# Three of eight experts' down products as three products of high and low parts

## The chip, the cores and the metric

The kernel runs on one core of a Trainium2 chip, as one launch. The time is the device time of that launch in microseconds (us). The core has five engines, each with a queue of its own that it works off in order: TensorE (PE in the profile, its weight loads PEld), VectorE (DVE), ScalarE (ACT), GpSimd (POOL) and SyncE (SP), which here issues DMA transfers. Engines wait for one another by semaphores.

## The reference

One transformer layer in float32: x has 8 sequences of 256 tokens of 128 features, 2048 tokens in all.

- Attention: 16 heads of 8 features, softmax over 256 keys, an output projection, added to x, layer norm: y.
- Feed-forward: a shared part, (silu(y sw1) * (y sw3)) sw2 with 256 hidden features, and a routed part. The router scores 8 experts by sigmoid(y router_w), takes the two best of each token and makes their scores sum to 1 (`comb`, zero for the other six). Each expert e is gelu(y ew1[e]) ew2[e], 128 by 128 and 128 by 128; the routed part is the sum over experts of comb[e] times that.
- y plus both parts, layer norm: the output.

Every expert is computed for every token; the gate `comb` is multiplied onto the hidden features before the second ("down") matrix.

## The kernel before, in words

**A written order.** `lay_out_slots` (L81) writes a list of slots, each with a list of jobs; every engine's program walks the same list and emits its own instructions for each job, so the list is the order in each engine's queue. The attention takes 64 slots with scores. What follows is the drain, which starts at about 135 us in the trace; "slot k" below is slot k of the drain (`NHALF + k` in the code), and "9 slots ahead of the drain" is `NHALF - 9`.

**Units.** The feed-forward works on groups of 512 tokens, g0 to g3, with features on the partitions. A unit is one group with one expert (g1E2: group 1, expert 2) or with one half of the shared hidden features. Slots 0 to 7 have two units each: g0E0 to g0E7, whose up products were made ahead of the drain, and, in this order, the shared halves of g0, g1 and g2, then g1E0 and g1E1. Slots 8 to 13 have g1E2 to g1E7, 14 and 15 the shared halves of g3, 16 to 23 g2E0 to g2E7, 24 to 29 g3E0 to g3E5, and 30 to 33 g3E6 and g3E7 by halves of 256 tokens.

**One expert unit.** TensorE makes the up product in a PSUM bank (`ring`, two in turn): three float32r products by `three` (L843), low weights with high activations, high with low, high with high. ScalarE takes gelu of it (L719), VectorE multiplies by the gates (L815) into one of four buffers `hid`, TensorE multiplies that by the down weights `wf` in float32 (L1050) and adds it to the group's accumulator in PSUM. For groups 0 to 2 this is one product of 512 columns; group 3's accumulator lies in two banks, so it is two of 256. The trace shows a float32 product as two instructions. The up product has to wait until gelu has read the unit that had its bank before, and `hid` until the down product of four units earlier is done.

**Where the down product stands.** For units of slots 0 to 7 in the next slot, after its up products; for the others two slots on, before that slot's up product.

**Jobs around it that the prediction names.**

- accT f, finT f, rstd2 f, norm2 f: group f is finished. ScalarE copies the accumulator (L726), TensorE transposes it (L1057) after that copy, VectorE adds y and makes the statistics (L822 to L829), GpSimd the reciprocal root (L574, L575), VectorE the normed output (L835), SP stores it. accT stands in slots 10, 16, 26, finT in 11, 17, 27, norm2 in 15, 21, 31 for f = 0, 1, 2; group 3 has two halves, f = 3 and 4, at the end. The statistics stand after the unit of their slot on VectorE.
- route, combT n, load gates n: group n's gates. GpSimd and VectorE make `comb`, TensorE transposes it (L1005), ScalarE copies it out of PSUM (L707), SP stores it to DRAM (L483) and loads it back, spread over all partitions, 2 MB (L478). combT stands in slots 7 and 18 and load gates in 8 and 19 for n = 2 and 3.
- ScalarE's exp (router, L701) needs another table than gelu and tanh: there are table loads before and after it, in slots 4 and 7.

`qstack` and `kstack` are the attention's operands and are not used in the drain.

Of the kernel before, what the change touches and what calls it, by code (L numbers as in the profile page):

```python
# [15 lines left out]
F32 = mybir.dt.float32  # L16
# [5 lines left out]
P = 128  # L22
# [39 lines left out]
WARM = 10  # L62

# [17 lines left out]
def lay_out_slots():  # L81
# [57 lines left out]
    for u, n in zip(EARLY, (53, 54, 55, 56, 58, 59, 61, 62)):  # L139
        put(n, ("up", u))  # L140

    for u in range(NUNITS):
        if UNIT_SLOT[u] >= NE:
            put(NHALF + UNIT_SLOT[u] + 2, ("down", u))
        put(NHALF + UNIT_SLOT[u], ("unit", u))
    for u in range(NUNITS):
        if UNIT_SLOT[u] < NE:
            put(NHALF + UNIT_SLOT[u] + 1, ("down", u))
# [49 lines left out]
def build_layer(nc, x, x_t, w_attn, w_first, b_first, b_rows, w_ffn, out):  # L198
    ctx = ExitStack()
    with ctx:  # L200
# [115 lines left out]
        up_copied = sem("up_copied")  # L316
        acc_taken, fin_stats, fin_rstd, fin_out = sem("acc_taken"), sem("fin_stats"), sem("fin_rstd"), sem("fin_out")
# [54 lines left out]
        def misc_of(u):  # L372
            return bank_of[u]

# [117 lines left out]
        def _(pool):  # L492
# [19 lines left out]
            for slot in slots:  # L512
                for kind, n in slot.jobs:
# [38 lines left out]
                    if kind == "add bo":  # L552
                        if n == 0:
                            wait_taken(pool, ("bo", 0))
                            pool.wait_ge(x_loaded, 16 * NG)
                        pool.tensor_tensor(xs[:, tiles(n), :], xs[:, tiles(n), :],
                                           bo_all[:, None, :].to_broadcast([P, TPG, P]), ALU.add).then_inc(xb_made, 1)
                    if kind == "y":
# [59 lines left out]
        def _(act):  # L618
# [10 lines left out]
            for slot in slots:  # L629
# [18 lines left out]
                for kind, b in slot.jobs:  # L648
# [59 lines left out]
                    if kind == "unit":  # L708
# [7 lines left out]
                        if b in SHARED:  # L716
                            nc.scalar.activation(act_out[:, b % 2, :], up[:, :], ACT.Tanh, scale=0.5).then_inc(act_made, 1)
                        else:
                            nc.scalar.activation(act_out[:, b % 2, c], up[:, c], ACT.Gelu).then_inc(act_made, 1)  # L719
                    if kind == "accT":  # L720
# [8 lines left out]
        def _(dve):  # L729
# [7 lines left out]
            for slot in slots:  # L737
# [10 lines left out]
                for kind, b in slot.jobs:  # L748
# [49 lines left out]
                    if kind == "unit":  # L798
# [13 lines left out]
                        else:  # L812
# [3 lines left out]
                                              gates_mem[:, g % 2, e * GT + c.start:e * GT + c.stop], ALU.mult).then_inc(hid_dve, 1)  # L816
                    if kind == "finT":
# [22 lines left out]
        def _(pe):  # L840
# [61 lines left out]
            for slot in slots:  # L902
# [25 lines left out]
                for kind, b in slot.jobs:  # L928
# [107 lines left out]
                    if kind == "down":  # L1036
# [10 lines left out]
                        if g == NG - 1 and b == first_of(g):  # L1047
                            pe.wait_ge(acc_taken, 1)
                        for bank, cols in acc_parts(g, cols_of(b)):
                            ins = mm(bank[:, cols], wf[:, c:c + P], hid[:, b % NHB, cols], start=b == first_of(g),  # L1050
# [52 lines left out]
```

## Time and profile before

| what | value |
|---|---|
| runs shown | 218.22, 219.63, 970.13 us; median 219.63 |
| profiled execution, its own time | 217.16 us |
| its span, first to last instruction | 215.3 us |
| mean granted clock of TensorE | 0.995 |
| busy: TensorE, VectorE, ScalarE, GpSimd | 93%, 72%, 64%, 60% of the span |
| chain that ended last, by engine | PE 66%, DVE 14%, POOL 6%, issue 5%, ACT 4% |

The profile is of one execution. Its own time is 1.9 us more than its span, which is what lies before the first and after the last instruction that is shown. One of the three runs took 970 us; the other two agree within 0.7%.

### The profile page before, as it was taken

The numbers are of one execution on the slowest core, as the hardware profiler recorded it, in microseconds if no ns is written. First come the engines' busy times: TensorE is split into PE (matmuls) and PEld (weight loads), VectorE is DVE, ScalarE is ACT, GpSimd is POOL, SyncE is SP. The second block draws the span as 40 slices with busy tenths as digits, with TensorE's granted clock in tenths as the row PEclk, the third lists the DMA queues.
The fourth block names the chain that finished last, engine by engine and source line by source line (L and its number), as shares of the span: only waits on it lengthen the run. The fifth ranks groups of instructions, "written<-read, shape, count | busy, mean of one in ns | idle before, by whom it ended". The sixth has DMA issues, their size and how long they took to land.

```text
span 215.3 us, 4566 instructions
## 1 busy us (share of the span) xinstructions
PE 201.1 (93%) x1564; PEld 118.5 (55%) x1564; DVE 155.1 (72%) x319; ACT 138.1 (64%) x280; POOL 128.8 (60%) x248
## 2 busy tenths in 40 slices
PE   7999999999999999999999999899999999999980
PEld 7765564444555555555555455556655656557750
DVE  6788888779898989999874343577582657663774
ACT  2799786887769778787886657734776424434330
POOL 8888999348679985975379344192570864300203
PEclk9999999999999999999999999999999999999998
DMA  4490474367420000000063002700003701290011
GB/s 139 129 270 24 109 228 114 87 198 257 110 68 9 0 9 2 9 0 3 6 243 161 3 0 84 313 0 0 0 0 88 307 0 36 65 386 6 0 52 49
DMA packets 10358, 19.19 MB, mean 89 GB/s; under 512 B 1920, under 2 KB 6912, under 8 KB 9696
## 3 DMA queue, kind: packets, MB, share of 16 engines
q1 hardware_dynamic: 8912, 17.06, 24.5%
q10 hardware_dynamic: 1040, 1.05, 1.5%
q0 software_dynamic: 384, 0.79, 1.4%
q8 instruction: 13, 0.21, 0.4%
q14 instruction: 9, 0.07, 0.1%
HBM read 12.80 MB, written 1.11 MB: 65 GB/s over the span
## 4 chain that ended last, share of the span: by engine, by line
PE 66%; DVE 14%; POOL 6%; issue 5%; ACT 4%; DMA 2%; POOLq 0%; DVEq 0%
PE pv_bank L893 11%; PE max_bank L1050 8%; PE ring L867 8%; DVE top L745 5%; PE sum_bank L1050 4%; PE sum_bank L867 3%; POOL qstack L428 3%; PE ring L845 2%; PE max_bank L876 2%; PE ring L847 2%; PE ring L846 2%; PE misc_bank L983 2%; PE pv_bank L901 2%; PE misc_bank L972 2%; PE misc_bank L845 2%
## 5 line engine op out<-in xcount | busy, mean ns | idle before, releaser
L745 DVE TENSOR_REDUCE top<-max_bank 128x2 f32<-128x512 f32 x128 | 80.6, 683 | 10.8 <-PE max_bank L876 10.8
L639 ACT ACTIVATE probs_mem<-ring 128x512 f32<-128x512 f32 x86 | 49.0, 599 | 15.7 <-PE ring L867 7.4
L876 PE MATMUL max_bank<-kstack,qstack 32*128 32x256 f32 x256 | 41.0, 328 | 0.3 <-DVE kstack L754 0.3
L893 PE MATMUL pv_bank<-probs_mem,v 128*18 128x256 f32 x512 | 40.1, 385 | 0.5 <-ACT probs_mem L639 0.2
L815 DVE TENSOR_TENSOR probs_mem<-xt,gates_mem 128x512 f32<-128x512 f32 (+1 forms) x34 | 22.7, 673 | 23.2 <-ACT xt L719 22.2
L867 PE MATMUL ring<-qstack,kstack 32*128 32x256 f32 x172 | 35.1, 326 | 1.7 <-DVE top L745 1.7
L639 ACT ACTIVATE probs_mem<-sum_bank 128x512 f32<-128x512 f32 x42 | 25.1, 598 | 7.5 <-PE ring L867 7.2
L719 ACT ACTIVATE xt<-ring 128x512 f32<-128x512 f32 (+1 forms) x26 | 14.7, 564 | 23.5 <-PE ring L847 23.5
L1050 PE MATMUL max_bank<-probs_mem,wf 128*128 128x512 f32 (+1 forms) x60 | 27.5, 541 | 1.3 <-DVE probs_mem L815 0.9
L876 PEld LDWEIGHTS max_bank<-kstack,qstack 32*128 32x128 f32 x256 | 25.4, 183 | 5.6 <-issue 2.5
L867 PEld LDWEIGHTS ring<-qstack,kstack 32*128 32x128 f32 x172 | 21.2, 183 | 13.3 <-issue 5.6
L845 PE MATMUL ring<-yt_hi,wf_lo 128*128 128x512 f32 (+1 forms) x34 | 22.0, 648 | 0.0
L867 PE MATMUL sum_bank<-qstack,kstack 32*128 32x256 f32 x84 | 20.7, 325 | 0.8 <-DVE top L745 0.4
L1050 PE MATMUL sum_bank<-probs_mem,wf 128*128 128x512 f32 (+1 forms) x40 | 15.9, 488 | 0.3 <-DVE probs_mem L815 0.3
L574 POOL TENSOR_SCALAR rstd<-mv 128x4 f32<-128x4 f32 (+1 forms) x5 | 1.9, 370 | 23.9 <-DVE mv L829 23.8
L867 PEld LDWEIGHTS sum_bank<-qstack,kstack 32*128 32x128 f32 x84 | 12.3, 183 | 6.1 <-ACT probs_mem L639 2.8
L569 POOL TENSOR_SCALAR yt_hi<-yt_raw 128x256 fp32r<-128x256 f32 x8 | 6.8, 852 | 13.1 <-ACT yt_raw L697 13.0
L1050 PEld LDWEIGHTS max_bank<-probs_mem,wf 128*128 128x128 f32 x60 | 9.7, 188 | 8.9 <-DVE probs_mem L815 4.4
L893 PEld LDWEIGHTS pv_bank<-probs_mem,v 128*18 128x18 f32 x512 | 8.6, 96 | 9.4 <-issue 0.7
L563 POOL TENSOR_SCALAR xs<-res,mv,rstd 128x128 f32<-128x128 f32 x16 | 12.7, 797 | 0.9
L847 PE MATMUL ring<-yt_hi,wf_hi 128*128 128x512 f32 (+1 forms) x34 | 13.0, 382 | 0.0
L846 PE MATMUL ring<-yt_lo,wf_hi 128*128 128x512 f32 (+1 forms) x34 | 13.0, 381 | 0.0
(183 smaller groups left out, 389.9 us busy)
## 6 DMA issues: line engine op xcount, KB each, us to landing
gates_mem<-gate_scratch SPq DMA_DIRECT2D x4, 2048.0 KB, 7.8
kstack<-gates_mem SPq DMA_DIRECT2D x36, 64.0 KB, 2.7
qstack<-gates_mem SPq DMA_DIRECT2D x24, 64.0 KB, 2.1
wf<-w_ffn_dram SPq DMA_DIRECT2D x1, 1408.0 KB, 7.3
xs<-x_dram SPq DMA_DIRECT2D x4, 256.0 KB, 5.6
xt<-x_t_dram SPq DMA_DIRECT2D x3, 256.0 KB, 4.4
qstack<-gates_mem POOLq DMA_DIRECT2D x12, 64.0 KB, 2.5
out_dram<-xs SPq DMA_DIRECT2D x3, 256.0 KB, 2.3
```

The lines of the kernel that those rows point to most:

```text
L563: ins = pool.tensor_scalar(xs[:, QT * n + t, :], res1[:, t, :], mv1[:, t, 0:1], rstd1[:, t:t + 1], ALU.subtract, ALU.mult)
L639: nc.scalar.activation(probs[:, i % 2, s_heads(s)[r], :], ring_of["scores", 2 * s + r][:, :], ACT.Exp, scale=SCALE).then_inc(probs_made, 1)
L719: nc.scalar.activation(act_out[:, b % 2, c], up[:, c], ACT.Gelu).then_inc(act_made, 1)
L745: dve.tensor_reduce(top[:, b % 2, m_heads(m)[r], t, :], max_bank[(2 * m + r) % NMAX][:, :].rearrange("p (h k) -> p h k", h=2), AX.X, ALU.m ...
L815: dve.tensor_tensor(hid[:, b % NHB, c], act_out[:, b % 2, c], gates_mem[:, g % 2, e * GT + c.start:e * GT + c.stop], ALU.mult).then_inc(hi ...
L845: mm(out_ap, w_lo, m_hi, start=first, stop=False)
L846: mm(out_ap, w_hi, m_lo, start=False, stop=False)
L847: return mm(out_ap, w_hi, m_hi, start=False, stop=last)
L867: ins = mm(ring_of["scores", 2 * s + r][:, kt * S:(kt + 1) * S], kstack[rows, t, k:k + P], qstack[rows, t, b * S:(b + 1) * S], start=True, ...
L876: ins = mm(max_bank[(2 * m + r) % NMAX][:, qt * S:(qt + 1) * S], qstack[rows, t, q:q + P], kstack[rows, t, b * S:(b + 1) * S], start=True, ...
L893: ins = mm(pv_bank[32 * j:32 * j + 2 * VW, 0:S], v[:, (QT * b + kt) * H // 2 + HPS * n + j, k * VW:(k + 2) * VW], probs[:, p // 2 % 2, j, ...
L1050: ins = mm(bank[:, cols], wf[:, c:c + P], hid[:, b % NHB, cols], start=b == first_of(g), stop=b in [fin_last(f) for f in range(len(FIN))])
```

## The change

Experts 0, 2 and 4 (`IN_PARTS`) are treated otherwise in all four groups, which makes twelve units (`PARTED`): slots 0, 2, 4 of g0; 6, 8, 10 of g1; 16, 18, 20 of g2; 24, 26, 28 of g3.

- Their down weights are split by GpSimd into a float32r high part and the rest, 128 columns for each expert, in three jobs ("split w2") 9, 7 and 5 slots ahead of the drain; the parts lie in `qstack`.
- Their hidden features are split too ("parts", after the last unit of the same slot): ScalarE waits for the gate product and copies it as float32r, VectorE waits for that copy and subtracts it from the product. The parts lie in `kstack`, two buffers in turn.
- Their down product is `three`: three float32r products in place of one in float32, per bank. TensorE waits for the subtraction before it.
- Their down product stands three slots on instead of two where it stood two on; in slots 1 to 7 it stands where it did.

```diff
@@ -60,6 +60,9 @@
 COPIES = ((1, 0, 0), (0, 0, 1))
 NC = 4
 WARM = 10
+
+IN_PARTS = (0, 2, 4)
+PARTED = tuple(u for u in range(NWHOLE) if UNITS[u][1] - NSH in IN_PARTS)
 
 SHIFT_D = (0, 4)
 NDIRECT = 2 * NT
@@ -138,11 +141,17 @@
                 put(first + 34 - 3 * (b // 2), ("load gates", b // 2))
     for u, n in zip(EARLY, (53, 54, 55, 56, 58, 59, 61, 62)):
         put(n, ("up", u))
+    for n in range(len(IN_PARTS)):
+        put(55 + 2 * n, ("split w2", n))
 
     for u in range(NUNITS):
         if UNIT_SLOT[u] >= NE:
-            put(NHALF + UNIT_SLOT[u] + 2, ("down", u))
+            put(NHALF + UNIT_SLOT[u] + (3 if u in PARTED else 2), ("down", u))
         put(NHALF + UNIT_SLOT[u], ("unit", u))
+        last = u if u + 1 == NUNITS or UNIT_SLOT[u + 1] > UNIT_SLOT[u] else None
+        for w in PARTED:
+            if last is not None and UNIT_SLOT[w] == UNIT_SLOT[last]:
+                put(NHALF + UNIT_SLOT[w], ("parts", w))
     for u in range(NUNITS):
         if UNIT_SLOT[u] < NE:
             put(NHALF + UNIT_SLOT[u] + 1, ("down", u))
@@ -314,6 +323,7 @@
         up_made, act_made, sh_read, hid_dve, down_made = (
             sem("up_made"), sem("act_made"), sem("sh_read"), sem("hid_dve"), sem("down_made"))
         up_copied = sem("up_copied")
+        w2_hi_made, w2_split, hid_hi_made, hid_lo_made = sem("w2_hi_made"), sem("w2_split"), sem("hid_hi_made"), sem("hid_lo_made")
         acc_taken, fin_stats, fin_rstd, fin_out = sem("acc_taken"), sem("fin_stats"), sem("fin_rstd"), sem("fin_out")
         out_stored = sem("out_stored")
 
@@ -371,6 +381,14 @@
 
         def misc_of(u):
             return bank_of[u]
+
+
+        def w2_part(e, i):
+            n = IN_PARTS.index(e)
+            return qstack[:, i, n * P:(n + 1) * P]
+
+        def hid_part(u, i):
+            return kstack[:, 2 * (PARTED.index(u) % 2) + i, 0:GT]
 
 
         def acc_parts(g, cols):
@@ -555,6 +573,14 @@
                             pool.wait_ge(x_loaded, 16 * NG)
                         pool.tensor_tensor(xs[:, tiles(n), :], xs[:, tiles(n), :],
                                            bo_all[:, None, :].to_broadcast([P, TPG, P]), ALU.add).then_inc(xb_made, 1)
+                    if kind == "split w2":
+                        if n == 0:
+                            pool.wait_ge(up_made, 1)
+                        e = IN_PARTS[n]
+                        c = slice(E2 + e * P, E2 + (e + 1) * P)
+                        pool.tensor_scalar(w2_part(e, 0), wf[:, c], 1.0, None, ALU.mult).then_inc(w2_hi_made, 1)
+                        pool.wait_ge(w2_hi_made, n + 1)
+                        pool.tensor_tensor(w2_part(e, 1), wf[:, c], w2_part(e, 0).bitcast(F32), ALU.subtract).then_inc(w2_split, 1)
                     if kind == "y":
                         pool.wait_ge(stats_made, n + 1)
                         chain(pool.tensor_scalar(rstd1[:, :], mv1[:, :, 1], EPS, None, ALU.add))
@@ -717,6 +743,12 @@
                             nc.scalar.activation(act_out[:, b % 2, :], up[:, :], ACT.Tanh, scale=0.5).then_inc(act_made, 1)
                         else:
                             nc.scalar.activation(act_out[:, b % 2, c], up[:, c], ACT.Gelu).then_inc(act_made, 1)
+                    if kind == "parts":
+                        n = PARTED.index(b)
+                        wait_hid(act, b)
+                        if n >= 2:
+                            act.wait_ge(down_made, PARTED[n - 2] + 1)
+                        nc.scalar.copy(hid_part(b, 0), hid[:, b % NHB, :]).then_inc(hid_hi_made, 1)
                     if kind == "accT":
                         g, t0, t1 = FIN[b]
                         act.wait_ge(down_made, fin_last(b) + 1)
@@ -814,6 +846,10 @@
                             e, c = n - NSH, cols_of(b)
                             dve.tensor_tensor(hid[:, b % NHB, c], act_out[:, b % 2, c],
                                               gates_mem[:, g % 2, e * GT + c.start:e * GT + c.stop], ALU.mult).then_inc(hid_dve, 1)
+                    if kind == "parts":
+                        dve.wait_ge(hid_hi_made, PARTED.index(b) + 1)
+                        dve.tensor_tensor(hid_part(b, 1), hid[:, b % NHB, :], hid_part(b, 0).bitcast(F32),
+                                          ALU.subtract).then_inc(hid_lo_made, 1)
                     if kind == "finT":
                         g, t0, t1 = FIN[b]
                         dve.wait_ge(misc_made, made[kind, b])
@@ -1046,7 +1082,15 @@
                         c = W2 + n * P
                         if g == NG - 1 and b == first_of(g):
                             pe.wait_ge(acc_taken, 1)
+                        if b in PARTED:
+                            e = n - NSH
+                            pe.wait_ge(w2_split, len(IN_PARTS))
+                            pe.wait_ge(hid_lo_made, PARTED.index(b) + 1)
                         for bank, cols in acc_parts(g, cols_of(b)):
+                            if b in PARTED:
+                                ins = three(bank[:, cols], w2_part(e, 0), w2_part(e, 1), hid_part(b, 0)[:, cols],
+                                            hid_part(b, 1)[:, cols], b == first_of(g), False)
+                                continue
                             ins = mm(bank[:, cols], wf[:, c:c + P], hid[:, b % NHB, cols], start=b == first_of(g),
                                      stop=b in [fin_last(f) for f in range(len(FIN))])
                         ins.then_inc(down_made, 1)
```

## Rows read from the trace of the kernel before

**Rows 1.** the page's busy time, share of the span and instructions.
```profile
PE 201.1 (93%) x1564; PEld 118.5 (55%) x1564; DVE 155.1 (72%) x319; ACT 138.1 (64%) x280; POOL 128.8 (60%) x248
```

**Rows 2.** stages: PE, PEld, DVE, ACT, POOL busy, then clock, DMA, GB/s.
```profile
190.00:200.00 10.00, 10.00 (x42) 6.72 (x41) 5.38 (x11) 4.06 (x7) 0.00 (x0) 1.00 0.35 134
...
210.00:215.30 5.30, 0.07 (x1) 0.00 (x0) 2.25 (x9) 0.00 (x0) 1.89 (x4) 0.82 0.17 49
```

**Rows 3.** chain of waits in the drain: start us, us, what.
```profile
149.34 0.23 PE ring L846
...
150.50 0.86 PE sum_bank L1050 x2
...
181.77 0.44 PE pv_bank L1057 x4
...
195.60 0.51 PE max_bank L1050 x2
...
196.11 0.43 PE sum_bank L1050 x2
...
204.00 0.12 PE ring L846
```

**Rows 4.** groups by line and shape, 135 to 208: busy us, mean ns.
```profile
L719 ACT ACTIVATE xt<-ring 128x512 f32<-128x512 f32 x22 | 13.1, 597 | 20.3 <-PE ring L847 20.2
...
L719 ACT ACTIVATE xt<-v 128x512 f32<-128x512 f32 x5 | 3.2, 630 | 0.6 <-DVE probs_mem L815 0.5
...
L726 ACT COPY xt<-max_bank 128x512 f32<-128x512 f32 x2 | 1.2, 580 | 0.0
```

**Rows 5.** gate product, by its line: duration ns min/median/max.
```profile
L815 DVE TENSOR_TENSOR probs_mem<-xt,gates_mem x34: 421/691/1222, 136.7 to 207.9; 128x512 f32<-128x512 f32 x30, 128x256 f32<-128x256 f32 x4
```

**Rows 6.** weight split's first instruction, by its line.
```profile
L532 POOL TENSOR_SCALAR wf_hi<-wf x16: 441/449/461, 53.3 to 79.8; 128x96 fp32r<-128x96 f32 x16
```

**Rows 7.** timeline of POOL ahead of the drain: start, us, idle before.
```profile
129.98 0.22 POOL L560 TENSOR_SCALAR rstd<-mv 128x2 f32<-128x2 f32 x1 [3.13 <-DVE mv L782]
```

**Rows 8.** timeline of ACT, slots 7 and 8: start, us.
```profile
158.21 0.63 ACT L719 ACTIVATE xt<-v 128x512 f32<-128x512 f32 x1 [0.54 <-DVE probs_mem L815]
...
159.98 1.28 ACT L701 ACT_TABLE_LOAD   x1
...
164.37 0.60 ACT L719 ACTIVATE xt<-ring 128x512 f32<-128x512 f32 x1
```

**Rows 9.** waits in the drain: us in total, times, longest.
```profile
PE max_bank L1050 <- DVE probs_mem L815: 0.9, 3, 0.4
```

**Rows 10.** timeline of ACT and DVE, slots 15 and 16.
```profile
180.23 0.58 ACT L726 COPY xt<-max_bank 128x512 f32<-128x512 f32 x1
...
180.31 1.09 DVE L835 TENSOR_SCALAR xs<-xt,mv,rstd 128x128 f32<-128x128 f32 x4
...
181.31 0.69 DVE L815 TENSOR_TENSOR probs_mem<-xt,gates_mem 128x512 f32<-128x512 f32 x1
```

**Rows 11.** timeline of DVE, ACT and SP, slots 17 to 24.
```profile
183.04 0.69 DVE L822 TENSOR_TENSOR xt<-pv_bank,xs 128x512 f32<-128x512 f32 x1
...
184.40 0.56 ACT L707 COPY comb_t<-misc_bank 8x512 f32<-8x512 f32 x1
...
184.97 0.66 DVE L815 TENSOR_TENSOR probs_mem<-xt,gates_mem 128x512 f32<-128x512 f32 x1
...
186.50 0.33 SPq L478 DMA_DIRECT2D gates_mem<-gate_scratch  x1
...
194.67 0.69 DVE L815 TENSOR_TENSOR probs_mem<-xt,gates_mem 128x512 f32<-128x512 f32 x1 [0.95 <-ACT xt L719]
```

**Rows 12.** stages: the slice in which the last gate load's traffic ends.
```profile
194.00:194.50 0.50, 0.50 (x3) 0.26 (x2) 0.00 (x0) 0.47 (x1) 0.00 (x0) 1.00 0.08 25
```

**Rows 13.** timeline of POOL and DVE, slot 6.
```profile
157.66 1.05 POOL L570 TENSOR_TENSOR yt_lo<-yt_raw,yt_hi 128x256 fp32r<-128x256 f32 x1
...
158.03 1.22 DVE L815 TENSOR_TENSOR probs_mem<-xt,gates_mem 128x512 f32<-128x512 f32 x1
```

## The prediction

> **What bounds the kernel now.** I read the page's busy time first [rows 1]: TensorE 93% of the span, no other engine above 72%. The table by stage [rows 2] shows where that holds in the stretch the change touches, the drain (135 us to the end): in 190 to 200 TensorE has no idle time, ScalarE works 4.1 us, VectorE 5.4, GpSimd nothing. The chain of waits [rows 3] then gives the size of a step, because it counts a pipelined product once: a float32 down product of 512 columns is 0.86 us, in group 3 (two halves) 0.51 + 0.43 = 0.94; a float32r product is 0.23 for 512 columns and 0.12 for 256. So TensorE's queue is what ends last, but with thin cover: a slot of the drain is one up product (0.70) and one down product (0.86), about 1.6 us, and in that time the unit's chain has to run gelu (0.60) and gate product (0.69) [rows 4, 5]: 1.3 us. Whatever is put between those two engines is put near the path.
>
> **The change, part by part.**
>
> *Removed from TensorE.* Twelve down products become three float32r products each. Nine (groups 0 to 2) go from 0.86 to 3 x 0.233 = 0.70: 9 x 0.16 = 1.4 us. Three (group 3) go from 0.94 to 6 x 0.117 = 0.70: 0.7 us. If TensorE never waited for it, 2.2 us. [rows 3]
>
> *Added.* ScalarE: 12 copies, SBUF to SBUF, 512 columns. The trace has a copy from PSUM at 0.58 and an activation from SBUF at 0.63 [rows 4]; I take 0.60, and 0.58 to 0.63 moves nothing. VectorE: 12 subtractions of two SBUF operands, as the gate product has them, whose median is 0.69 and whose longest is 1.22 [rows 5]; I take the median and keep the longest as the upper end. GpSimd: three weight splits of two instructions; a 96-column one takes 0.45 [rows 6], so 2 x 0.45 x 128/96 = 1.2 us a split. They stand 9, 7 and 5 slots ahead of the drain, before the last batch's normalisation, where GpSimd waits 3.13 us [rows 7]; TensorE asks for them only in the drain. I cost them at nothing; if all three fell into that one gap they would overrun it by 0.5 us, which is the upper end. No DMA is added.
>
> *Moved.* From slot 8 on the parted unit's down product stands in slot +3, so even slots have one up product and no down product, odd slots two. The hidden buffer is reused four units later, after that slot: no wait. The new wait on TensorE is for the subtraction. The wait that matters is the other one: **ScalarE waits for the gate product before its copy, in the middle of its queue**, and behind the copy stand the next gelu, and in slots 10, 16 and 26 the copy of a finished accumulator (accT), in slot 18 the copy of the last group's gates (combT 3). TensorE's transposes (finT) wait for the first, the gate load for the second.
>
> I carried the four queues forward slot by slot, with 0.60 for ScalarE, 0.69 for VectorE, 0.03 to 0.05 for a hand-over and 0.5 or 0.6 for two independent instructions back to back. Where it stands against before:
>
> a) Slots 0 to 7. Both up products of a slot (1.4 us) precede the downs, so copy and subtraction are hidden; three parted units give 0.45 us. In slot 6 half goes back: g1E0's copy can start only after its gate product (about 159.1), ending at 159.7; then gelu g0E7 (158.21 before), gelu g1E1 (two at 0.5 pitch), a table load of 1.28, exp (0.2), the gate copy (0.6) and a second load of 1.28 follow on ScalarE, with hand-overs 4.4 us, and gelu g1E2 comes at 164.1 against 164.37 [rows 8]. Standing: -0.2 us.
>
> b) Slots 8 to 14. g1E2: gelu to 164.7, gate product 165.5, copy 166.1, subtraction 166.8; TensorE is there at 166.0 and idles 0.8. accT 0 behind g1E4's copy costs 0.3. Against that 0.3 of saved products and two of the three old waits of 0.9 together [rows 9]. Standing: +0.1.
>
> c) Slot 17. VectorE norms group 0 at 180.31 for 1.09 us, so g2E0's gate product comes at 181.31 already today, and ends at 182.0 [rows 10]. accT 1, today at 180.23, must now follow the copy behind that: 181.4 + 0.69, copy to 182.7, accT to 183.2. finT 1 was issued at 181.77 [rows 3]; TensorE arrives at 181.85 and waits until 183.27. This is the clearest single cost: 1.4 us. Standing: +1.5.
>
> d) Slots 18 to 24. finT 1's residual and statistics take VectorE from 183.04 to 184.97 [rows 11] and stand before g2E2's gate product; its copy and subtraction end 1.4 us after that. TensorE waits about 0.5 and 0.35, and regains 0.5 by three cheaper products and 0.2 in bubbles. Standing: +1.6.
>
> e) The last gates. combT 3's copy stands behind g2E2's copy, which waits for (d): 187.5 instead of 184.40, 3.1 us later. Store and load follow: the load goes out at 186.50 and its traffic ends in the slice 194.0 to 194.5 [rows 11, 12]; the first product that reads it starts at 194.67, 0.4 us of slack. The load moves 3.1, the stream only 1.6: 3.1 - 1.6 - 0.4 = 1.1 us. Standing: +2.7.
>
> f) Slots 24 to the end. accT 2's wait stays hidden behind the late gates. finT 2's 1.93 us on VectorE stand before g3E4's gate product, copy and subtraction: TensorE idles 1.35 in slot 31, 0.3 elsewhere, and saves 0.7. Standing at the end: **+3.6 us**.
>
> The profiled execution took 217.16 us, so it would take 220.8. The median of the runs shown, 219.63, lies 2.5 above the profiled run and the lowest 1.1 above; with the middle, 1.8, I forecast 222.5.
>
> **A rule against the trace.** The longest gate product, 1.22 us, began at 158.03, inside a GpSimd subtraction that ran from 157.66 for 1.05 [rows 13]; the median met no such thing, so in the sum each subtraction is 0.69. The Trainium skill (SBUF — State Buffer, section Who interferes with whom) says that a VectorE instruction with two SBUF inputs and a GpSimd instruction that reads SBUF shut each other out: the second to issue waits for the first. By that rule, which these two rows agree with, the subtractions of slots 6 to 20 are all exposed; with 0.5 us more for each of the three of slots 16 to 20 alone the sum would be an estimated +5.1 in place of +3.6.
>
> **Rivals.**
>
> *The ScalarE-VectorE loop becomes the bound (ends slower).* For a pair of slots the loop is gate product, copy, subtraction, gate product: 3 x 0.69 + 0.60 and hand-overs, 2.8 us; TensorE's pair is 0.70 + 0.86 + 2 x 0.70 = 2.96. It decides when one step costs 0.2 us more than I took. A subtraction blocked as in [rows 13] costs 0.5 more; over six pairs of groups 2 and 3, with 0.3 us lost in each, 2 us: +5.6, or 224.6. For it: the margin is 5%. Against it: GpSimd does nothing in 190 to 200 [rows 2], so only slots 16 to 21 are exposed. Chance 0.20.
>
> *All savings are collected.* 217.16 - 2.2 = 215.0, as a median 216.8. For it: TensorE is the bound by every view, and slots 0 to 5 hide the additions. Against it: (c) needs no assumption on prices, only the order on ScalarE. Chance 0.10.
>
> *Only the waits of (b) and (c) stay.* If combT 3's copy slips by less than 2 us the gates arrive in time, and the finer waits vanish in the slots without a down product: about +1.5, 220.5. Chance 0.20.
>
> *TensorE's clock.* The granted clock is 1.00 in the drain and 0.82 only in the last slice, where TensorE hardly works [rows 2]; new idle stretches are at most 1.4 us. If it fell there, 3 us of products at half speed would cost 3 more: 225.5. Chance 0.05.
>
> **How the numbers follow.** Forecast 0.45, its own range +1.5 to +5.5 us, 219.7 to 225.1 with the two offsets. The range down to the third rival and most of the second, up to the first and the clock: 218.2 to 226.3. What this kernel's measurement can tell from no change is about 2%, 4.4 us. Faster by more than that is out of reach of 2.2 us of savings: 0.02. Slower: the first rival and the clock, and a quarter of the forecast's own chance: 0.33. Within: 0.65.
>
> **What would show it.** In the profile after: parted downs as three L845 to L847-like products of 0.23 (else the saving is wrong); ScalarE's copies beginning just after a gate product, and accT 1 after one; idle time of TensorE before finT 1 of a microsecond or more, named for ScalarE (if under 0.3, (c) is wrong); the last gate load issued near 189.6 and a gate product waiting for it (if issued before 188, (e) is wrong); TensorE's idle time before the parted downs of g1E2 and g3E4 named for VectorE. A shorter span than 215 us would refute the whole reading.

## The result, and the profile after

The changed kernel took 223.14 us (median of six runs) where the kernel before took 218.17 on the same chip: ratio 1.0204, 95% interval 1.0158 to 1.0251, so 3.4 to 5.5 us slower. The ratio leaves out the executions at a lower granted clock (two of the six, 225.70 and 227.65 us), so it is not the quotient of the two medians. The forecast was 222.5, of which the last step, from the profiled execution to a median, was 0.8 too large: before's median lay 1.0 above its profiled run here, not 1.8. The work itself was forecast at +3.6. The interval of the runs contains that; the two profiled executions, compared below, show more.

The spans differ by 5.9 us, but not all of that is the change's. ScalarE's first tanh of the drain starts at 136.99 us before and at 137.78 after. That start varied from 136.72 to 139.11 over the kernels below, and did not follow the edits: e5 and e10 run the same code up to there and start at 139.11 and 136.72. From there to the end of the span it is 78.3 us before and 83.4 after: **the drain is 5.1 us longer**. All lengths of the drain below are counted this way.

The page's busy time, and two stages of the table by stage (columns as in [rows 2]), of the changed kernel:

```profile
PE 201.2 (91%) x1579; PEld 120.5 (54%) x1579; DVE 163.2 (74%) x331; ACT 144.2 (65%) x292; POOL 132.9 (60%) x254
...
190.00:200.00 10.00, 9.71 (x32) 5.63 (x32) 5.82 (x12) 4.06 (x8) 0.00 (x0) 1.00 0.65 238
210.00:221.20 11.20, 4.95 (x27) 3.53 (x25) 5.62 (x21) 1.79 (x5) 1.89 (x4) 0.90 0.16 47
```

Against [rows 1, 2]: the granted clock is 1.00 in every stage from 140 to 210, as it was before, so the clock is not it. TensorE's busy time did not fall, although its products got shorter: a float32r product of 512 columns counts about 0.39 in busy time and 0.23 in the chain. The chain of waits of the changed kernel, from g2E0's gate product to g3E0's down product, the first in three products in group 3 (start us, us, what):

```profile
183.28 0.61 DVE probs_mem L847
183.92 0.02 ACT kstack L751
184.44 0.58 ACT xt L758
185.02 0.51 ACT xt L745
...
186.16 0.70 DVE xt L858
...
189.31 0.57 ACT comb_t L733
...
191.41 7.54 DMA gates_mem<-gate_scratch
199.07 0.70 DVE probs_mem L847
...
201.64 0.12 PE max_bank L882
```

Where TensorE carried this stretch of the chain before [rows 3], VectorE, ScalarE and the gate load carry it now. L751 is ScalarE's copy of the high part, L758 accT, L745 gelu, L733 the copy of combT, L847 the gate product, L851 the subtraction, L858 finT's addition of y. The timeline of ScalarE for units g2E0 and g2E1 (slots 16 and 17), with the idle time before an instruction and its releaser in brackets:

```profile
181.62 0.60 ACT L745 ACTIVATE xt<-ring 128x512 f32<-128x512 f32 x1 [1.29 <-PE ring L883]
183.92 0.62 ACT L751 CAST kstack<-probs_mem 128x512 fp32r<-128x512 f32 x1 [1.70 <-DVE probs_mem L847]
184.44 0.58 ACT L758 COPY xt<-max_bank 128x512 f32<-128x512 f32 x1
184.92 0.60 ACT L745 ACTIVATE xt<-ring 128x512 f32<-128x512 f32 x1
```

The copy stands idle 1.70 us in the middle of ScalarE's queue for a gate product that is itself behind VectorE's norm of group 0; accT 1 and the next gelu stand behind it. The second gelu waits for no one: its up product had ended 1.3 us before, at 183.65. Before, gelu g2E1 started at 181.81 and had waited for TensorE. The waits of the drain, us in total, times, longest, first of the changed kernel, then two of the kernel before:

```profile
ACT xt L745 <- PE ring L883: 12.8, 12, 2.3
ACT kstack L751 <- DVE probs_mem L847: 12.4, 10, 2.1
DVE kstack L851 <- ACT kstack L751: 6.2, 9, 0.7
PE max_bank L881 <- DVE kstack L851: 5.0, 5, 1.6
PE pv_bank L1101 <- ACT xt L758: 2.1, 2, 1.5
DVE probs_mem L847 <- DMA gates_mem<-gate_scratch: 1.5, 1, 1.5
```
```profile
ACT xt L719 <- PE ring L847: 23.5, 24, 1.5
PEld max_bank L1050 <- DVE probs_mem L815: 4.4, 12, 0.8
```

A gelu that waits for its up product is in time: 24 were before, 12 are now. The last row, of the kernel before, is one that the prediction missed: before the change TensorE's weight loads for the down products already waited 12 times, 4.4 us, for the gate product. [rows 9] shows only the part of it that is booked on the products themselves, 0.9.

### The profile page after: what moved, and what is told of

Same layout as the page of the kernel before. It is cut to its first block, busy times and chain, and to the rows that moved or that the text cites. A ratio compares the mean times of both kernels' runs of the same rounds, so it can differ in the third digit from the quotient of the medians.

```text
span 221.2 us, 4648 instructions
## 1 busy us (share of the span) xinstructions
PE 201.2 (91%) x1579; PEld 120.5 (54%) x1579; DVE 163.2 (74%) x331; ACT 144.2 (65%) x292; POOL 132.9 (60%) x254
## 3 DMA queue, kind: packets, MB, share of 16 engines
q10 hardware_dynamic: 1040, 1.05, 1.4%
## 4 chain that ended last, share of the span: by engine, by line
PE 59%; DVE 20%; ACT 9%; issue 6%; DMA 3%; ACTq 1%; POOLq 0%; POOL 0%; DVEq 0%
PE pv_bank L929 12%; PE ring L903 8%; DVE top L777 5%; DMA gates_mem<-gate_scratch 3%; DVE probs_mem L847 3%; PE sum_bank L903 3%; PE max_bank L912 3%; PE pv_bank L937 2%; PE sum_bank L1094 2%; PE misc_bank L1019 2%; PE max_bank L1094 2%; PE max_bank L881 2%; ACT xt L745 2%; PE ring L980 2%; PE misc_bank L1008 2%
## 5 line engine op out<-in xcount | busy, mean ns | idle before, releaser
L847 DVE TENSOR_TENSOR probs_mem<-xt,gates_mem 128x512 f32<-128x512 f32 (+1 forms) x34 | 22.5, 675 | 15.4 <-ACT xt L745 13.9
L745 ACT ACTIVATE xt<-ring 128x512 f32<-128x512 f32 (+1 forms) x26 | 14.2, 561 | 13.5 <-PE ring L883 12.8
L1094 PE MATMUL max_bank<-probs_mem,wf 128*128 128x512 f32 (+1 forms) x42 | 19.3, 540 | 0.9 <-DVE probs_mem L847 0.6
L881 PE MATMUL ring<-yt_hi,wf_lo 128*128 128x512 f32 (+1 forms) x34 | 19.7, 579 | 0.0
L751 ACT CAST kstack<-probs_mem 128x512 fp32r<-128x512 f32 x12 | 7.4, 618 | 12.4 <-DVE probs_mem L847 12.4
L851 DVE TENSOR_TENSOR kstack<-probs_mem,kstack 128x512 fp32r<-128x512 f32 x12 | 8.4, 702 | 6.2 <-ACT kstack L751 6.2
```

The costliest lines, as they stand in the source:

```text
L847: dve.tensor_tensor(hid[:, b % NHB, c], act_out[:, b % 2, c], gates_mem[:, g % 2, e * GT + c.start:e * GT + c.stop], ALU.mult).then_inc(hi ...
L881: mm(out_ap, w_lo, m_hi, start=first, stop=False)
```

## The experiments

One table for all. "At" is the start of a unit's gelu or tanh in ScalarE's timeline, minus its start before, both counted from the first tanh of the drain; "end" is the same for the end of the span. So a column shows how late the stream runs there, and the step between two columns is what that stretch cost.

| kernel | ratio to before (95%) | at g1E0 | g1E2 | g3, 1st shared | g2E3 | g3E0 | g3E4 | end |
|---|---|---|---|---|---|---|---|---|
| changed | 1.0204 (1.0158 to 1.0251) | 0.08 | 0.37 | 1.09 | 3.09 | 3.05 | 3.32 | 5.1 |
| e1 parts last | 1.021 (1.0173 to 1.0247) | 0.85 | 1.08 | 1.82 | 2.98 | 3.19 | 2.86 | 4.7 |
| e2 products only | 0.9938 (0.9899 to 0.9976) | -0.32 | -0.73 | -0.89 | -1.05 | -1.08 | -1.20 | -1.15 |
| e3 no last gates | 1.0233 (1.0205 to 1.026) | 0.11 | 0.38 | 1.09 | 3.08 | 3.05 | 2.76 | 4.6 |
| e4 pairs later | 1.0075 (1.0041 to 1.0108) | 0.86 | 0.61 | 0.83 | 2.32 | 1.98 | 1.64 | 2.05 |
| e5 parts unused | 1.0228 (1.0166 to 1.0291) | 0.44 | 0.11 | 0.93 | 2.95 | 2.91 | 4.46 | 4.8 |
| e6 parts next | 1.0176 (1.0097 to 1.0255) | 0.85 | 0.80 | 2.74 | 1.57 | 4.22 | 4.09 | 4.0 |
| e7 copy on VectorE | 1.0125 (1.0073 to 1.0177) | 0.29 | 0.53 | 0.91 | 1.71 | 2.30 | 1.81 | 3.4 |
| e8 only g0 | 0.9964 (0.9927 to 1.0001) | 0.09 | -0.40 | -0.38 | -0.35 | -0.38 | -0.39 | -0.3 |
| e9 subtraction only | 1.002 (0.9978 to 1.0061) | 0.03 | 0.25 | 0.36 | 0.40 | 0.60 | 0.56 | 0.8 |
| e10 copy only | 1.0185 (1.0134 to 1.0236) | 0.44 | 0.11 | 0.93 | 2.95 | 2.91 | 4.53 | 4.8 |
| e11 pairs later, parts last from slot 8 | 1.0021 (0.999 to 1.0052) | 0.08 | -0.11 | 0.11 | 1.59 | 1.24 | 0.91 | 1.2 |
| e12 the same, copy on VectorE | 1.0005 (0.9968 to 1.0042) | 0.30 | 0.53 | 0.58 | -0.14 | 1.03 | 0.60 | 0.4 |

The last column comes from one profiled execution each, the ratio from several runs. Taken times 218 us, each ratio's excess lies within 0.9 us of the last column; differences of 0.5 us are read from the columns, not from the ratios.

**e1, the parts behind accT and combT.**

```diff
+    for slot in slots:
+        slot.jobs.sort(key=lambda job: job[0] == "parts")
```

> Edit: within a slot the two instructions that make the parts go to the end of the slot's list, behind accT 0 to 2 and the copy of combT 3; nothing else is changed. Theory (written order on ScalarE): the copy of the high part waits 1.6 us for a gate product, and accT 1, then finT 1, and the copy of combT 3 with the last gates' load stand behind it; freed of that, finT 1 waits nothing (1.5 less) and the last load is issued 2 to 3 us earlier, so the wait of 1.5 us on it goes: 2.0 to 2.5 us faster than the changed kernel, about 220.7 us where the kernel before takes 218.2 (ratio 1.01). Rival (the twelve subtractions' and copies' hand-over between ScalarE and VectorE costs by itself, whatever stands behind it): within 0.5 us of the changed kernel, ratio 1.018 to 1.022.

Measured: ratio 1.021, as slow as the changed kernel; drain 0.4 shorter. My first theory, 2.0 to 2.5 us, was far too large. Its waits:

```profile
PE max_bank L883 <- DVE kstack L853: 5.3, 5, 1.6
PE pv_bank L1103 <- ACT xt L760: 0.6, 1, 0.6
```

finT's wait for accT did go, 2.1 to 0.6 us, and with it the stretch from the g3 units to g2E3 costs 1.2 in place of 2.0. But in the slots 0 to 5 the parts now stand behind the attention's last jobs and come late there: +0.77 at g1E0. TensorE's waits for the subtraction stayed (5.3 against 5.0). The edit took one wait off the stream and put another on.

**e2, the products without the parts.**

```diff
-            put(NHALF + UNIT_SLOT[u] + (3 if u in PARTED else 2), ("down", u))
+            put(NHALF + UNIT_SLOT[u] + 2, ("down", u))
...
-                put(NHALF + UNIT_SLOT[w], ("parts", w))
...
-                            pe.wait_ge(hid_lo_made, PARTED.index(b) + 1)
```

> Leaves out the making of the parts in the drain (the products read what lies in the tiles, so the sums are not the reference's); the twelve down products are still three products each and stand two slots behind their unit, as the float32 ones did. It shows what TensorE alone gains. Theory: 2.2 us faster than the kernel before (9 times 0.16 and 3 times 0.24), as TensorE waits little there: about 216.0 us, ratio 0.990. Rival (the three products save nothing, since TensorE's busy time in the drain did not shrink in the changed kernel, 201.2 against 201.1 us): ratio 1.00, and then waits alone did not cause the loss.

Measured: ratio 0.9938, drain 1.15 shorter. The products are cheaper, but only half of 2.2 us is collected. It comes in g0 and g1 (-1.08 at g1E7); the six units of g2 and g3 bring 0.1 to 0.3. Starts of TensorE's second instruction of each up product in slots 20 to 23, of e2 and then of before:

```profile
186.87 0.40 PE L881 MATMUL ring<-yt_lo,wf_hi 128*128 128x512 f32 x1
188.48 0.40 PE L881 MATMUL ring<-yt_lo,wf_hi 128*128 128x512 f32 x1
189.94 0.40 PE L881 MATMUL ring<-yt_lo,wf_hi 128*128 128x512 f32 x1
191.72 0.40 PE L881 MATMUL ring<-yt_lo,wf_hi 128*128 128x512 f32 x1
```
```profile
186.88 0.40 PE L846 MATMUL ring<-yt_lo,wf_hi 128*128 128x512 f32 x1
188.48 0.40 PE L846 MATMUL ring<-yt_lo,wf_hi 128*128 128x512 f32 x1
190.12 0.40 PE L846 MATMUL ring<-yt_lo,wf_hi 128*128 128x512 f32 x1
191.72 0.40 PE L846 MATMUL ring<-yt_lo,wf_hi 128*128 128x512 f32 x1
```

The slot with the parted product is 1.46 us in place of 1.64, the next one 1.78 in place of 1.60: the 0.18 goes into waiting for the next gate product. So before the change two slots of g2, 3.2 us, were as long as TensorE's work in them and, within 0.2 us, as long as the round of up product, gelu, gate product and down product, which also takes two slots.

**e3, no load of the last gates.**

```diff
+                        if n == NG - 1:
+                            continue
...
-                            dve.wait_ge(gates_loaded[g % 2], 16 * (g // 2 + 1))
+                            dve.wait_ge(gates_loaded[g % 2], 16 * (min(g, 1) // 2 + 1) if g != 2 else 32)
```

> Leaves out the load of the last group's gates and the wait for it: the last group is weighted with the gates of group 1. Theory: VectorE's wait of 1.51 us for that load before g3E0's gate product is lost time, so 1.2 to 1.5 us less than the changed kernel: ratio to the kernel before 1.014. Rival (something else is as late there, the copy of g2E4's part or accT 1): the gate product waits for its gelu instead and the end moves by under 0.4 us: ratio 1.019 to 1.021.

Measured: ratio 1.0233, no gain; in the table the stream is 0.57 earlier from g3E1 on and 0.5 at the end. The load's wait of 1.51 is in the trace, but only 0.5 of it is on the path: without it g3E0's gate product waits for the copies and gelus that are late anyway. That is the rival, nearly to its number (under 0.4).

**e4, the downs of a pair one slot later.** As e1, and:

```diff
-            put(NHALF + UNIT_SLOT[u] + (3 if u in PARTED else 2), ("down", u))
+            put(NHALF + UNIT_SLOT[u] + (4 if u in PARTED else 3 if u - 1 in PARTED else 2), ("down", u))
...
-            put(NHALF + UNIT_SLOT[u] + 1, ("down", u))
+            put(NHALF + UNIT_SLOT[u] + (2 if u in PARTED and u not in EARLY else 1), ("down", u))
```

> Edit: the parts at the end of their slot as in the first kernel of this set, and the down products of a parted unit, and of the unit behind it, one slot later still (g1E0's too). Theory: TensorE then also stops waiting for VectorE's subtraction in the drain (five waits of 5.0 us together in the changed kernel), of which some 3 us are on the path: 3 us beyond the first kernel of this set, about 217 to 218 us, ratio 0.995 to 1.0. Rival (ScalarE and VectorE are the bound with the parts in, so waits only move to the gelus and the gate products): no better than the first kernel of this set by more than 0.5 us, ratio 1.008 or above.

Measured: ratio 1.0075, drain 2.65 shorter than e1's. That is nearly the 3 us of the theory, from a level that was 2 us higher than the theory's. TensorE's five waits for the subtraction (5.3) are gone, one of 0.4 is left, and a new one comes in:

```profile
ACT kstack L753 <- DVE probs_mem L849: 10.4, 9, 2.4
PE ring L883 <- ACT xt L747: 2.4, 4, 1.3
PE sum_bank L883 <- DVE kstack L853: 0.4, 1, 0.4
```

The up product now waits for a bank that a late gelu has not read yet. ScalarE's copy still waits 10.4 us for gate products.

**e5, the parts made and not used.** TensorE's code is that of before:

```diff
-            put(NHALF + UNIT_SLOT[u] + (3 if u in PARTED else 2), ("down", u))
+            put(NHALF + UNIT_SLOT[u] + 2, ("down", u))
...
-                        if b in PARTED:
+                        if False:
...
```

> The parts are made as in the changed kernel, in the same places of ScalarE's and VectorE's lists, but nobody reads them: the twelve down products are the float32 ones of before, two slots behind their unit, and wait for the gate product alone. Theory now (the two instructions per unit hold up the next gelu and the next gate product on their own engines, since ScalarE's copy waits for a gate product and VectorE's subtraction for that copy): most of the loss stays, ratio to the kernel before 1.012 to 1.020. Rival (the loss is TensorE's waiting for the subtraction, five waits of 5.0 us): with nobody waiting for it, 1.000 to 1.004.

Measured: ratio 1.0228, drain 4.8 longer. **Nearly the whole loss is there while nobody waits for a part.** So most of it needs no waiting of TensorE for the subtraction, though these five waits are TensorE's largest by name in the changed kernel. It comes from what stands in ScalarE's and VectorE's queues. That does not make the five waits free: e5 gives up the cheaper products too. The parts alone cost 4.8 and the products alone save 1.15 (e2), which makes +3.65; the changed kernel stands at +5.1. The 1.5 between belongs to neither alone. TensorE's waits for the parts, which only the changed kernel has, are its likely cause; that is not shown.

**e6, the parts one slot later.** As e4, and the jobs go behind the next unit:

```diff
-                put(NHALF + UNIT_SLOT[w], ("parts", w))
+                put(NHALF + UNIT_SLOT[w] + (w not in EARLY), ("parts", w))
```

> Edit: from slot 6 of the drain on, the copy and the subtraction of a unit stand one slot later, behind the gelu and the gate product of the next unit, and the downs as in the fourth kernel (both of a pair four slots behind the first). The work is the same. Theory (an engine that waits in order for the other is what costs): ScalarE's copy finds its gate product made and VectorE's subtraction does not hold up the next gate product; 1.5 to 2.5 us faster than the fourth kernel (1.0075), ratio 0.996 to 1.001. Rival (the added busy time, 7.4 us of ScalarE and 8.4 us of VectorE, is itself the cost): no better than the fourth kernel, 1.006 to 1.009.

Measured: ratio 1.0176, slower than e4 (1.0075). ScalarE's waits for a gate product ahead of its copies fell from 10.4 to 1.2 us, and it did not help: that theory, as I put it, fell. The table says where: 1.9 us of the difference to e4 are there by the g3 units. The chain of waits of e6:

```profile
163.26 0.02 ACT comb_t L735
...
163.75 0.62 ACT kstack L753
164.39 0.70 DVE kstack L853
...
165.23 0.47 PE max_bank L883
```

g1E0's copy, at the end of slot 7, now stands behind the copy of group 2's gates, which waits for GpSimd's routing. From there to the end e6 and e4 lose the same, 1.3 and 1.2. So up to the g3 units this run compares another place with another neighbour. Behind them ScalarE's copies wait 7.5 us in e4 and 0.9 in e6, for the same loss: with the downs where both kernels have them, these waits by themselves do not set the pace.

**e7, VectorE makes both parts.**

```diff
-                        nc.scalar.copy(hid_part(b, 0), hid[:, b % NHB, :]).then_inc(hid_hi_made, 1)
...
+                        dve.tensor_scalar(hid_part(b, 0), hid[:, b % NHB, :], 1.0, None, ALU.mult).then_inc(hid_hi_made, 1)
```

> Edit: VectorE makes the high part too (a copy with rounding ahead of its subtraction), ScalarE has no part in it; places in the lists and slots as in the changed kernel. Theory (the hand-over is the cost): VectorE's waits for ScalarE's copy (6.2 us in 9 waits) and ScalarE's waits for the gate product (12.4 us) go, the gelus stand as before, and VectorE has some 0.35 to 0.7 us more per unit: ratio 1.005 to 1.014. Rival (VectorE's own work ahead of the next gate product is the cost): it grows by 12 times 0.35 to 0.7 us, ratio 1.022 to 1.035.

Measured: ratio 1.0125, drain 1.7 shorter than the changed kernel's, with 5.2 us more work on VectorE (12 copies of 0.43). It is work for the busier engine, but ScalarE no longer waits in mid-queue for a gate product of its own unit. finT's wait for accT is 0.6 again, as before the change. TensorE still waits 3.9 us for the subtraction.

**e8, group 0 alone.**

```diff
-PARTED = tuple(u for u in range(NWHOLE) if UNITS[u][1] - NSH in IN_PARTS)
+PARTED = tuple(u for u in range(NWHOLE) if UNITS[u][1] - NSH in IN_PARTS and UNITS[u][0] == 0)
```

> Edit: only the three units of group 0 are in three products (slots 0, 2 and 4 of the drain, where two units share a slot and the parts stand behind both); the other nine are as before. Theory: TensorE never waits for a part there in the changed kernel's trace, so the saving of three units stays: 3 times 0.16, ratio 0.998. Rival (two instructions per unit cost 0.2 us or more each wherever they stand): ratio 1.001 to 1.004.

Measured: ratio 0.9964, interval to 1.0001; drain 0.3 shorter. In slots 0 to 5, with two up products each, the parts are hidden. This is the only kernel with the parts that comes out ahead of the one before, and by less than the interval can settle.

**e9 and e10, one engine at a time.** Both as e5. e9 leaves ScalarE's copies out and lets VectorE wait for the gate product alone; e10 leaves VectorE's subtractions out.

```diff
e9
...
-                        nc.scalar.copy(hid_part(b, 0), hid[:, b % NHB, :]).then_inc(hid_hi_made, 1)
...
-                        dve.wait_ge(hid_hi_made, PARTED.index(b) + 1)
+                        wait_hid(dve, b)
e10
-                        dve.tensor_tensor(hid_part(b, 1), hid[:, b % NHB, :], hid_part(b, 0).bitcast(F32),
-                                          ALU.subtract).then_inc(hid_lo_made, 1)
```

> As the fifth kernel (parts made, products float32 and two slots behind), without ScalarE's copies: VectorE alone has its twelve subtractions, which wait for no other engine. It leaves out the high parts. Theory (each engine's added work delays the next unit by its own size, and the two add up): the subtraction, 0.70 us ahead of the next gate product, makes somewhat more than half of the fifth kernel's loss (1.0228), ratio 1.010 to 1.015. Rival (it is the hand-over, a copy that waits for a gate product and a subtraction that waits for the copy; busy time alone hides): ratio 1.000 to 1.005.

> As the fifth kernel, without VectorE's subtractions: ScalarE alone has its twelve copies, each behind its unit's gate product, with the next gelu behind it. It leaves out the low parts. Theory: the next gelu comes up to 1.3 us later (0.7 for the gate product, 0.63 for the copy) where TensorE has it ready, ratio 1.006 to 1.012. Rival A (the hand-over both ways makes the loss): at or under 1.004. Rival B (the copy alone makes all of it): 1.018 to 1.024.

Measured: e9 1.002, drain +0.8; e10 1.0185, drain +4.8, the same as e5 in every column within 0.1. **The copy alone makes the whole loss of e5, the subtraction alone little, and the two do not add up.** The subtraction costs 0.8 alone, and nothing on top of the copy. That refutes "each by its own size" and is e10's rival B. Waits of e9 and then of e10:

```profile
ACT xt L745 <- PE ring L879: 23.8, 24, 1.5
PE pv_bank L1097 <- ACT xt L754: 0.6, 1, 0.6
```
```profile
ACT xt L745 <- PE ring L881: 16.2, 15, 1.9
ACT kstack L751 <- DVE probs_mem L847: 9.1, 10, 1.7
PE pv_bank L1099 <- ACT xt L758: 2.8, 3, 1.5
PE misc_bank L1099 <- ACT xt L758: 0.8, 1, 0.8
```

With the subtraction alone 24 gelus are in time, as before the change; with the copy alone 15, and finT's waits for accT are 3.6 us in place of 0.6. ScalarE has room for the copies: it works 3.5 to 5.1 us in each 10 of the changed kernel's stages from 170 to 210. But a copy that first waits for VectorE takes none of that room. What stands behind it, a gelu, an accT or a combT, starts only after the gate product and the copy. The chain of waits of e10 shows it, for accT 1 and for combT 3:

```profile
182.08 0.61 DVE probs_mem L847
...
182.71 0.02 ACT kstack L751
...
183.24 0.58 ACT xt L758
...
187.57 0.02 ACT kstack L751
...
188.10 0.58 ACT comb_t L733
```

The chain passes through six of the twelve copies in this way. Each time about 0.55 us lie between the end of the gate product and the start of the next instruction on ScalarE, 3.3 us in all, and the gate product itself lies on the chain too. So the copy's own time does count there; it is the wait ahead of it that puts it on the path. That the same copy without a wait would have cost next to nothing is argued, from e9's subtraction of 0.69 us: no kernel has such a copy.

**e11, the schedule mended.** As e4, with the sort of e1 from slot 8 on only.

```diff
+    for s in range(NHALF + NE, NHALF + len(SERIES) + 12):
+        at[s].jobs.sort(key=lambda job: job[0] == "parts")
```

> Edit: as the fourth kernel, but the parts go to the end of the list in the slots from 8 on alone; in slots 0 to 7 they stay where the change put them. Theory: in the fourth kernel the gelu of g1E0 stood 0.85 us late against 0.08 in the changed kernel, because the parts came behind the other work of the slots 0 to 7, and this 0.77 is carried to the end: drain 1.3 us longer than before, ratio 1.004. Rival (the next waits give it back): as the fourth kernel, 1.0075.

Measured: ratio 1.0021, drain +1.24, as forecast for the drain and a little better in the runs. The 0.77 of the early slots is carried to the end (2.05 to 1.24). ScalarE's copies wait as long as ever:

```profile
ACT kstack L753 <- DVE probs_mem L849: 10.6, 10, 2.4
```

**e12, and the copy on VectorE.**

> Edit: as the kernel just before, with VectorE making the high part too. Theory: what the copy on VectorE gained in the seventh kernel against the changed kernel (1.7 us) is in part the same wait that the later downs hide; 0.5 to 1.0 us faster than the kernel just before, ratio 0.999 to 1.002. Rival (VectorE, with 0.44 us more per unit, is then the engine that gives the pace): slower than the kernel just before, 1.007 or above.

Measured: ratio 1.0005, interval 0.9968 to 1.0042; drain +0.4. In the profiles 0.84 better than e11, as expected; the two ratios' intervals overlap, so the runs alone do not show it. Of its waits,

```profile
ACT xt L747 <- PE ring L886: 19.2, 13, 2.6
PE sum_bank L884 <- DVE kstack L854: 0.2, 1, 0.2
```

TensorE's for the subtraction are nearly gone. Three edits to the order and the engine take 4.7 of the 5.1 us out again with all twelve units in three products. If the saving is the 1.15 of e2 here too, waits of 1.55 us remain.

The changed kernel (+5.1), e7 (+3.4), e11 (+1.2) and e12 (+0.4) make a square. Moving the copy to VectorE is worth 1.7 us where the downs stand as in the changed kernel, and 0.8 where they stand later. The later downs, with accT and combT ahead of the copy from slot 8 on, are worth 3.9 us with the copy on ScalarE and 3.0 with it on VectorE. So the 4.8 us of e10 are no fixed price of the copy: they are its price while TensorE asks for the down product two slots behind the unit and accT stands behind the copy. With the second edit the copies still wait 10.6 us, and most of it no longer costs.

## Why the prediction was right, and where it was not

**The mechanism.** ScalarE waiting for the gate product "in the middle of its queue", ahead of the next gelu, accT and combT, was a wait that matters: the copy alone costs 4.8 us (e10), an instruction of like length on VectorE 0.8 (e9). The Trainium skill (PSUM — Partial Sum Buffer, section Engine vs sequencer instructions) calls the queues of ScalarE, VectorE and GpSimd strictly first in, first out; the trace agrees: the gelu at 184.92 had its product at 183.65 and still stood behind the copy.

**The sum.** Forecast +3.6, which is 5.8 of waits less 2.2 saved. Measured +5.1, which is 6.3 less 1.15 (e2). So the mis-sized term is first of all **the saving: "if TensorE never waited for it, 2.2 us"**, of which 1.15 was there to be had; the other 0.5 is in the waits. That the saving is the same with the waits in is assumed. Part of the closeness to the measured time is luck: the offset from the profiled run to a median was 0.8 too large and made up for about half of the 1.5 that the work was forecast too small. The prices of the products were right (0.23 and 0.12 in the chain). The condition was not: I read TensorE's idle time from its products [rows 9] and its full busy time in 190 to 200 [rows 2], not from its weight loads, which waited 4.4 us for gate products. Cheaper products make such a wait longer: in e2 the same waits of the weight loads are 5.4 us in 13, and 1.2 in place of 0.9 on the products.

By the forecast's own stations, the start at 137.78 taken out:

| station | forecast | measured |
|---|---|---|
| (a) gelu g1E2 | -0.2 | +0.4 |
| (b) to slot 14 | +0.1 | +1.1 |
| (c) behind finT 1 (end of g2E3's up product, 189.02 against 185.86) | +1.5 | +2.4 |
| (e) g3E0's gate product, 199.07 against 194.67 | +2.7 | +3.6 |
| (f) end | +3.6 | +5.1 |

- (a) was 0.6 short. TensorE waited 0.94 us for g1E0's part, which I had hidden; one VectorE instruction ahead of its gate product, below, is part of it.
- (b) was 0.7 in place of 0.3. Only TensorE's wait for g1E2's part (0.8 forecast, 0.96 in the trace) and accT 0 behind g1E4's copy (0.3) were priced; the later gelus behind the two copies were not.
- (c) held: finT 1 waited 1.52 for accT 1, 1.4 forecast, step 1.3. But as a price it is no property of accT: e1 let accT go first, and the subtraction's wait took most of the time back.
- (d), (e): step 1.2 as forecast. The load was issued at 191.41, 4.1 later in the stream (3.1 forecast), and the gate product waited 1.51. Yet with the load gone 0.5 is won (e3), not 1.1: the term's sum came out, but its cause only by half, so that the step fits is in part luck.
- (f) was 1.5 in place of 0.9: TensorE waited 1.56 for g3E4's part (1.35 forecast), but also 1.15 for g3E0's, where I had 0.3 for all the rest.
- GpSimd's splits show no cost, as forecast. They took 1.0 us each, and GpSimd still waited 1.04 ahead of the last batch's normalisation. No kernel but the one before is without them, so this is not shown by a run of its own.

**The rivals.** Nearest came "the loop becomes the bound", +5.6, for its size. Its condition was a subtraction blocked by GpSimd; the twelve subtractions took 0.684 to 0.834 us, median 0.692, so it did not occur there. The loop was tight for another reason, the order on ScalarE. The +5.1 that the prediction worked out by the rule on blocked subtractions equals the measured drain by luck, since its half microsecond on each did not occur either. None of the three subtractions of slots 16 to 20 took longer than 0.69 us, not even the one that by the profile began inside a GpSimd instruction with two inputs:

```profile
188.92 1.04 POOL L601 TENSOR_TENSOR rstd<-rstd,minus_half 128x4 f32<-128x4 f32 x1
```
```profile
189.43 0.69 DVE L851 TENSOR_TENSOR kstack<-probs_mem,kstack 128x512 fp32r<-128x512 f32 x1 [0.69 <-ACT kstack L751]
```

"All savings are collected" and "only the waits of (b) and (c) stay" are out, and so is the clock (granted 1.00 until 210).

What stays open: how the 4.8 us of e10 divide among the gelus, accT and combT that the copy holds back. The table narrows it: the steps are 0.8 from g1E2 to the first shared unit of g3 (accT 0), 2.0 from there to g2E3 (accT 1 and combT 3) and 1.6 from g3E0 to g3E4 (accT 2). But each of these stretches also has a gelu behind a copy, and e1, which let accT and combT go first, won only 0.4 with TensorE's waits in place. No kernel held back just one, and e10 with accT first was not run.

## What to carry to other kernels

Before an instruction goes into an in-order queue, ask what it waits for and who stands behind it. Two remedies worked here. One is to give it to the engine that makes its input, even the busier one (e7 against the changed kernel: 1.7 us). The other was worth more: to let what waits behind go first and the consumer ask a slot later, so that the delay is hidden (e11 against the changed kernel: 3.9 us). A saving on the engine that bounds is worth only what its next operand, seen at the weight load too, leaves of it. And two runs take such a change apart: the new work made and not used (e5), and the new use without the work (e2); moving single victims of a wait out of its way (e1, e3) only shows the next one.

## What was not expected of the hardware

A VectorE instruction of four elements can take as long as one of 512. Timeline of VectorE and of GpSimd in slot 6 of the changed kernel:

```profile
157.98 0.70 DVE L825 TENSOR_SCALAR den_inv<-den 128x4 f32<-128x4 f32 x1
```
```profile
157.93 0.73 POOL L596 TENSOR_TENSOR yt_lo<-yt_raw,yt_hi 128x256 fp32r<-128x256 f32 x1
```

Four elements with one input tensor took 0.70 us, and ended as GpSimd's subtraction did; the other three of that line took 0.17. The Trainium skill (SBUF — State Buffer, section Who interferes with whom) has tensor_scalar, when its operands meet certain conditions, among the operations that can take both of VectorE's ports and then shut GpSimd out or are shut out. This one row agrees. That the port was what held it is not shown otherwise.

The same rounding copy of 512 columns took 0.62 us on ScalarE (L751 above) and 0.43 on VectorE in e7:

```profile
L850 DVE TENSOR_SCALAR kstack<-probs_mem 128x512 fp32r<-128x512 f32 x12 | 5.2, 435 | 0.3
```
